# GpSimd's bulk loads of two attentions as single transfers in another order

## The reference

```python
# x: (8, 32, 32, 192), 12 heads of 16
x = x + conv_attn(group_norm(x))      # attention over all 1024 positions of an image:
#   scores = (q * scale) k^T + rel_h[..., :, None] + rel_w[..., None, :], softmax, times v, projection
t = x as tokens (8, 1024, 192)
t = t + attn(layer_norm(t))           # q k^T / sqrt(192), softmax, times v; 12 heads
t = t + ffn(layer_norm(t))            # each token by the expert of 16 with the largest logit
```

## Time and profile before

| what | us |
|---|---|
| median of 3 runs | 3230.5 (3227.85 to 3234.65) |
| span of the profiled execution | 3278.2 |
| PE busy | 2922.2 (89%) |
| DVE busy | 2439.8 (74%) |
| ACT busy | 1849.7 (56%) |
| POOL busy | 1061.6 (32%) |

### The profile page before, as it was taken

The page is one execution under the profiler, slowest core; times in us unless marked ns, Lnnn a source line. Parts: engine busy times, 40 slices in busy tenths (PEclk is TensorE's granted clock), DMA queues, the critical chain, the costliest instruction groups (busy, mean ns, idle before and its releaser), DMA issues. The chain is left out here.

```text
span 3278.2 us, 63755 instructions
## 1 busy us (share of the span) xinstructions
PE 2922.2 (89%) x17818; PEld 1147.0 (35%) x17818; DVE 2439.8 (74%) x4430; ACT 1849.7 (56%) x2379; POOL 1061.6 (32%) x1714
## 2 busy tenths in 40 slices
PE   5886999999999999977897999999999999871887
PEld 4664122222222222215652222222222222361666
DVE  4544899999999999933547999999999999451221
ACT  2433376667776677663440677777777777610332
POOL 0012233333333333213232333232333332155665
PEclk9776799999999999998995999999999999965777
DMA  6776554555445554433654622222222222350211
GB/s 126 219 237 184 104 103 98 100 110 107 102 101 100 111 103 100 90 61 121 206 160 98 124 72 70 72 75 75 73 76 75 70 71 63 97 89 12 58 54 35
DMA packets 222364, 327.92 MB, mean 100 GB/s; under 512 B 63820, under 2 KB 150550, under 8 KB 217650
## 3 DMA queue, kind: packets, MB, share of 16 engines
q0 software_dynamic: 79488, 202.00, 27.3%
q1 hardware_dynamic: 142772, 124.60, 14.5%
HBM read 217.71 MB, written 109.19 MB: 100 GB/s over the span
## 5 line engine op out<-in xcount | busy, mean ns | idle before, releaser
L458 ACT ACTIVATE a_probs<-a_psS 128x1024 f32<-128x1024 f32 x1536 | 1488.5, 1021 | 738.5 <-PE a_psS L371 734.0
L503 DVE TENSOR_REDUCE h_halfmax<-a_psR 128x1 f32<-128x512 f32 x1536 | 979.7, 686 | 73.5 <-PE a_psR L353 64.3
L503 DVE TENSOR_REDUCE a_halfmax<-a_psR 128x1 f32<-128x512 f32 x1536 | 984.2, 686 | 63.6 <-PE a_psR L353 54.5
L371 PE MATMUL a_psS<-a_qrows,a_krows 121*128 121x512 f16 (+1 forms) x3072 | 804.2, 383 | 44.8 <-DMA a_qrows<-relh 40.2
L382 PE MATMUL a_psO<-a_probs,a_v 128*32 128x512 f32 x6144 | 824.0, 609 | 1.2 <-ACT a_probs L458 1.2
L353 PE MATMUL a_psR<-h_kmax,h_qmax 64*128 64x512 f16 x1536 | 357.9, 405 | 40.8 <-POOL h_ident L39 40.1
L371 PEld LDWEIGHTS a_psS<-a_qrows,a_krows 121*128 121x128 f16 (+1 forms) x3072 | 241.8, 98 | 417.7 <-issue 161.5
L353 PE MATMUL a_psR<-a_kmax,a_qmax 64*128 64x512 f16 x1536 | 325.6, 393 | 1.8 <-DVE a_halfmax L503 1.4
L353 PEld LDWEIGHTS a_psR<-h_kmax,h_qmax 64*128 64x128 f16 x1536 | 81.9, 93 | 539.1 <-DVE h_halfmax L503 471.6
L353 PEld LDWEIGHTS a_psR<-a_kmax,a_qmax 64*128 64x128 f16 x1536 | 78.9, 93 | 490.4 <-DVE a_halfmax L503 460.1
L185 POOL DMA_DIRECT2D a_qrows<-qk x240 | 124.1, 517 | 264.5 <-PE a_psO L382 262.0
(11 more groups left out here) (185 smaller groups left out, 2755.2 us busy)
## 6 DMA issues: line engine op xcount, KB each, us to landing
a_qrows<-qk POOLq DMA_DIRECT2D x240, 128.0 KB, 4.2
qk<-p_half SPq DMA_DIRECT2D x96, 256.0 KB, 3.3
a_qrows<-rel POOLq DMA_DIRECT2D x96, 256.0 KB, 4.2
a_v<-v POOLq DMA_DIRECT2D x96, 256.0 KB, 3.1
a_krows<-qk POOLq DMA_DIRECT2D x168, 128.0 KB, 4.5
v<-p_v SPq DMA_DIRECT2D x36, 512.0 KB, 5.7
relh<-p_rel SPq DMA_DIRECT2D x48, 256.0 KB
attn<-a_out SPq DMA_DIRECT2D x96, 128.0 KB, 2.3
```

What stands on the lines that cost most here:

```text
L371: mm = nc.tensor.matmul(psS[:, (2 * n + j) % 4, :], K[buf][:, h, keys], A[buf][kt % NA][:, h, queries], start=True, stop=True)
L458: nc.scalar.activation(PT[:, blk % 2, 2 * pair:2 * pair + 2, :], psS[:, b0:b0 + 2, :], ACT.Exp, scale=scale).then_inc(exped, 1)
L503: nc.vector.tensor_reduce(mx[:, unit, half:half + 1], psR[:, slot, :], AX.X, ALU.max)\
```

## The change

The helpers that issued several transfers are split into one for each transfer, and `load_maxima` and `load` call them in another order, spread over more blocks. The transfers, their sizes, their semaphores and what PE waits for stay as they are.

| block | a1 before | a1 after | a2 before | a2 after |
|---|---|---|---|---|
| 0, 1 | 4, 2 maxima | 2 queries (L185 before) each | 2 maxima | 1 maxima query, 1 query or key |
| 2 | 2 maxima | 2 maxima, 2 queries | 2 maxima | as above |
| 3, 4 | 3 maxima | 2 maxima, 1 width | 2 maxima | as above |
| 5 | 3 terms | 2 maxima, 1 width | 2 maxima | as above |
| 6 | 3 terms | 1 maxima key, 1 width | 2 maxima | as above |
| 7 | 3 terms | 1 maxima key, 2 keys | 2 maxima | as above |
| 8 | 1 width, 1 height | 1 maxima width, 1 key, 2 heights | 1 query, 1 key | 2 maxima keys |
| 9 | 1 width, 1 height | 1 maxima width | 1 query, 1 key | 2 maxima keys |
| 10, 11 | 1 width | 1 maxima width | 1 query, 1 key | 2 maxima keys |
| 12, 13 | V | V | V | V |

```diff
@@ GpSimd of attention
-            def load_terms(s, buf, n):
+            def load_query(s, buf, c, n):
                 at = slice(HD * n, HD * n + HD)
-                for c in range(NA):
-                    pool.dma_start(A[buf][c][at, :, :], qk(s, TERMS[n][0], 0)).then_inc(loaded[buf], 16)
+                pool.dma_start(A[buf][c][at, :, :], qk(s, TERMS[n][0], 0)).then_inc(loaded[buf], 16)
+
+            def load_key(s, buf, n):
+                at = slice(HD * n, HD * n + HD)
                 pool.dma_start(K[buf][at, :, :], qk(s, TERMS[n][1], 1)).then_inc(loaded[buf], 16)
...
             def load_maxima(s, buf, blk):
 
+                if rel and 2 <= blk < 6:
+                    load_max_query(s, buf, blk % 2, (blk - 2) // 2, 0)
+                    load_max_height(s, buf, blk % 2, (blk - 2) // 2)
+                elif rel and blk in (6, 7):
+                    load_max_key(s, buf, blk % 2, 0)
+                elif rel and 8 <= blk < 12:
+                    load_max_width(s, buf, blk % 2, (blk - 8) // 2)
+                if not rel and blk < 8:
+                    load_max_query(s, buf, blk % 2, 0, blk // 2)
+                elif not rel and 8 <= blk < 12:
+                    load_max_key(s, buf, 0, blk - 8)
+                    load_max_key(s, buf, 1, blk - 8)
+
+            def load(s, buf, blk):
+
                 if rel:
-                    if blk == 0:
-                        load_max_terms(s, buf, 0, 0)
-                        load_max_terms(s, buf, 1, 0)
-                    elif blk < 5:
-                        load_max_rel(s, buf, blk % 2, (blk - 1) // 2)
+                    if blk < 3:
+                        load_query(s, buf, 0, blk)
+                        load_query(s, buf, 1, blk)
+                    elif blk < 7:
+                        load_width(s, buf, blk % 2, (blk - 3) // 2)
+                    elif blk == 7:
+                        load_key(s, buf, 0)
+                        load_key(s, buf, 1)
+                    elif blk == 8:
+                        load_key(s, buf, 2)
+                        load_height(s, buf, 0)
+                        load_height(s, buf, 1)
                 elif blk < 8:
-                    load_max_terms(s, buf, blk % 2, blk // 2)
-
-            def load(s, buf, blk):
-
-                if rel:
-                    if blk in (5, 6, 7):
-                        load_terms(s, buf, blk - 5)
-                    elif blk in (8, 9, 10, 11):
-                        load_rel(s, buf, blk % 2, (blk - 8) // 2)
-                elif blk in (8, 9, 10, 11):
-                    load_terms(s, buf, blk - 8)
+                    (load_query(s, buf, 0, blk // 2) if blk % 2 == 0 else load_key(s, buf, blk // 2))
                 if blk in (12, 13):
                     load_values(s, buf, blk - 12)
 
             make_identity(nc, pool, ident, const_done)
             for blk in range(12):
                 load(0, 0, blk)
-            for blk in range(BLK):
+            for blk in range(12):
                 load_maxima(1, 1, blk)
```

More of the change, by code:

```diff
@@ L181, in _, with load_width, load_height @@
         def _(pool):
-            def load_terms(s, buf, n):
+            def load_query(s, buf, c, n):
                 at = slice(HD * n, HD * n + HD)
-                for c in range(NA):
-                    pool.dma_start(A[buf][c][at, :, :], qk(s, TERMS[n][0], 0)).then_inc(loaded[buf], 16)
+                pool.dma_start(A[buf][c][at, :, :], qk(s, TERMS[n][0], 0)).then_inc(loaded[buf], 16)
+            def load_key(s, buf, n):
+                at = slice(HD * n, HD * n + HD)
                 pool.dma_start(K[buf][at, :, :], qk(s, TERMS[n][1], 1)).then_inc(loaded[buf], 16)
-            def load_rel(s, buf, c, half):
-                w, h = QR + WI * half, RH + 4 * half
+            def load_width(s, buf, c, half):
+                w = QR + WI * half
                 pool.dma_start(A[buf][c][w:w + WI, :, :], rel_w(s, half)).then_inc(loaded[buf], 16)
-                if half == 0:
-                    pool.dma_start(A[buf][c][RH:RH + 8, :, :], RLH[s, c].rearrange("i (k h) t -> (i k) h t", h=GH))\
-                        .then_inc(loaded[buf], 16)
+            def load_height(s, buf, c):
+                pool.dma_start(A[buf][c][RH:RH + 8, :, :], RLH[s, c].rearrange("i (k h) t -> (i k) h t", h=GH))\
+                    .then_inc(loaded[buf], 16)
             def load_values(s, buf, part):
@@ L197, in load_values, with load_max_query, load_max_key, load_max_width @@
                 pool.dma_start(V[buf][:, x, :, :], VN[s][:, x, :, :]).then_inc(loaded[buf], 16)
-            def load_max_terms(s, buf, r, n):
+            def load_max_query(s, buf, r, half, n):
                 of = slice(64 * r + HD * n, 64 * r + HD * n + HD)
-                pool.dma_start(AM[buf][0][of, :, :], qk_pair(s, TERMS[n][0], 0, r)).then_inc(loadedm[buf], 16)
+                pool.dma_start(AM[buf][half][of, :, :], qk_pair(s, TERMS[n][0], 0, r)).then_inc(loadedm[buf], 16)
+            def load_max_key(s, buf, r, n):
+                of = slice(64 * r + HD * n, 64 * r + HD * n + HD)
                 pool.dma_start(KM[buf][of, :, :], qk_pair(s, TERMS[n][1], 1, r)).then_inc(loadedm[buf], 16)
[L204 to L210, removed]
+            def load_max_width(s, buf, r, half):
+                of = slice(64 * r + HD, 64 * r + HD + WI)
+                pool.dma_start(AM[buf][half][of, :, :], RL[s, 0].rearrange("(k r p) t -> r k p t", p=2, r=2)[r])\
+                    .then_inc(loadedm[buf], 16)
+            def load_max_height(s, buf, r, half):
+                of = slice(64 * r + HD + WI, 64 * r + 64)
+                pool.dma_start(AM[buf][half][of, :, :],
                                RLH[s].rearrange("x i (k r p) t -> i r x k (p t)", p=2, r=2)[0, r, 4 * half:4 * half + 4])\
@@ L214, in load_maxima @@
             def load_maxima(s, buf, blk):
-                if rel:
-                    if blk == 0:
-                        load_max_terms(s, buf, 0, 0)
-                        load_max_terms(s, buf, 1, 0)
-                    elif blk < 5:
-                        load_max_rel(s, buf, blk % 2, (blk - 1) // 2)
-                elif blk < 8:
-                    load_max_terms(s, buf, blk % 2, blk // 2)
+                if rel and 2 <= blk < 6:
[10 more added lines that the diff above has]
+                    load_max_key(s, buf, 1, blk - 8)
             def load(s, buf, blk):
                 if rel:
-                    if blk in (5, 6, 7):
-                        load_terms(s, buf, blk - 5)
-                    elif blk in (8, 9, 10, 11):
-                        load_rel(s, buf, blk % 2, (blk - 8) // 2)
-                elif blk in (8, 9, 10, 11):
-                    load_terms(s, buf, blk - 8)
+                    if blk < 3:
[10 more added lines that the diff above has]
+                        load_height(s, buf, 1)
+                elif blk < 8:
+                    (load_query(s, buf, 0, blk // 2) if blk % 2 == 0 else load_key(s, buf, blk // 2))
                 if blk in (12, 13):
```

## The result

| | us |
|---|---|
| before, 4 runs beside it | 3229.8 (3227.9 to 3234.7) |
| after, 4 runs | 3263.7 (3257.3 to 3268.1) |
| ratio | 1.010 (1.0085 to 1.0116) |

The changed kernel is 34 us slower. Forecast were 23 us less; the time lies outside the range, and on the other side.

The account below looks back on a forecast made before the run. TensorE, busy nearly throughout both attentions, was taken as the bound, with a1 losing a height-row wait each step. Terms -48 + 6.6 + 15.4 + 3 = -23 us took 3230.5 to 3207.5 us, range 3186 to 3240.

Parts of the forecast that it names:

- Item 1: In a1, the scores' whole wait for the height rows goes: -48 us, bounds -40.2 and -48.
- The reading: Row transfers in a1 land 2.6 us after issue or 0.3 us after the last bulk load issued before, whichever is later.
- the table of landings per block: In a1, rows land 3.6 to 3.8 us after issue against 4.0, or at most 4.3 against 4.6.
- One reading: In a1, POOL's loads of blocks 7 and 8 were placed about 0.5 us after the scores of their own block.
- Item 2: Maxima's loads in a1, moved to blocks 2 to 11, delay block 13's scores 0.3 us a step: +6.6 us.
- Item 3: In a2, block 11's second maxima key load lands 0.7 us late for block 13: +15.4 us, plus +3 in weights' steps.
- the 3 us: In a2's steps 0 and 1, the experts' weights make the last maxima load later by 1.1 us more: +3 us.
- POOL isn't late anywhere: In both attentions, POOL's largest group, four loads, issues for 2.2 us of a 2.61 us block, so it costs nothing.
- the 2.15 us from block 11's first load to its deadline: Time from POOL's first load of block 11 to block 13's scores, read in a2 and used for a1 too.
- A: Rival: the maxima's loads at block 13 do not hurt, leaving the gain: 3182 to 3198 us; chance 0.10.
- B: Rival: a1's row transfers take turns with bulk packets in every busy block: +18 us, 3226 us; chance 0.17.
- C: Rival: a1's backlog survives until block 8, so the row wait stays: 3255.5 us; chance 0.16.

Follow-up runs that it names:

- e9: Before's order, with a1's three third-term loads moved from block 7 to blocks 11, 12 and 13: 3186.8 us, ratio 0.9859.
- e11: e4 with a1's two query loads of block 2 moved to block 6 and block 6's width load to block 9: 3236.5 us, ratio 1.0016.
- e5: Before's order, with a1's three third-term loads moved from block 7 to blocks 11, 12 and 14: 3197.5 us, ratio 0.9886.
- e8: e4 with a1's bulk width loads of blocks 3, 4 and 5 moved to blocks 9, 12 and 14: 3249.2 us, ratio 1.0056.
- e4: e1 with a1's last maxima width load moved from block 11 to block 10: 3210.2 us, ratio 0.9944.
- e1: After's order in a1 alone, before's order in a2: 3219.7 us, ratio 0.9956.
- e2: After's order in a2 alone, before's order in a1: 3266.7 us, ratio 1.0112.
- e7: e6 with one large a2 key load also moved from block 7 to block 12: 3241.1 us, ratio 1.003.
- e10: Before's orders, with the last of a2's maxima loads issued in block 12 instead of 7: 3348.6 us, ratio 1.0364.
- e6: e2 with one of block 11's two a2 maxima key loads moved to block 10: 3241.4 us, ratio 1.0018.

## Why the prediction was wrong, by its own steps

**Item 1, the height rows (-48 us): mis-sized, the mechanism right for the kernel before.** The price was right: e9 gets 47.8 us. It isn't the price of the waits alone, though. Where bare waits of 40.2 us stood against 46.2, the clock was in between: in before's a1 the granted clock fell to half for 3.4 us behind four of the 23 waits, as in step 3, behind a wait of 2.40 us:

```profile
536.70:540.10 3.40, 3.40 (x17) 1.19 (x16) 2.13 (x4) 1.34 (x2) 0.50 (x1) 0.50 0.24 55
```

Step 15, with a fall and a wait as long as its neighbours', is 1.2 us longer than they are, so the four are worth some 5 us (an estimate from that one step). The other profiles with the old order in a1 have three to seven such falls; e9 and after have none.

The reading was that a row transfer lands about 2.6 us after its issue, or 0.3 us behind the last bulk load issued before it. The first half holds (2.4 to 2.7 us with a light queue), the second where there is a backlog: the medians are 0.2 us in before's block 10 and 0.3 in e11's block 12 (landings read from the updates of the rows' semaphore in the trace). In after it was too short: the rows for blocks 5, 6, 7 and 11 landed 0.7, 1.9, 0.5 and 1.6 us behind that load. At block 11 of step 5 even a load issued 0.3 us behind the rows landed 1.2 us before them, so the order of issue isn't the whole rule; what the rest is, no run here shows.

The step that failed is therefore the table of landings per block. It set 3.6 to 3.8 us against a limit of 4.0, and at most 4.3 against 4.6, and called the whole wait gone. Measured medians of the rows issued in blocks 3, 5 and 9 were 4.24, 4.26 and 4.67 us, over their limits of 4.0, 4.0 and 4.6; those issued in block 8, where 3.8 stood, took 3.45. In step 5 the query load went out 0.15 us later behind the block's first load than assumed and the rows 0.1 earlier; the load took 3.8 us where 3.7 (3.5 and 0.2) stood, and the rows landed 0.4 us behind it where 0.3 stood: 4.2 us in place of 3.7. Tenths of a us decided, and margins of 0.2 to 0.4 us had been counted as certain.

The second part is the pause: the earlier trace rows show one step, and the trace of before has the pause ahead of block 1's loads in every third step. In before it costs nothing: five of the seven steps with it take 45.3 to 45.8 us, like the others, and the other two are those with a fall of the clock. In after such a step takes 1.16 us more (46.40 against 45.24 us), since the six loads of blocks 1 and 2 and the three of block 3 then come in a row; the rows issued in block 4, 3.7 us in the median, take up to 6.0. What is left of the 48 us: 27.7 in row waits and 8 in item 2's waits leave some 12, and a1 got 11 shorter, 4 of them by less waiting and the rest mostly by the four falls.

One reading was off without harm to the sum: loads of blocks 7 and 8 stand half a us behind the scores of blocks 8 and 9, not of their own block. e5 and e8 paid for it.

**Item 2, a1's maxima (+6.6 us): right.** The scores of block 13 cost 6.6 us over 21 steps, 9.4 at block 13 of which block 14 made up 2.8; e4 moved one load and got 5.9 back.

**Item 3, a2's maxima (+15.4 and +3 us): right for the ordinary step, wrong as a sum.** Ordinary steps lost 0.64 us, 14 us over 22 of them. The weights' steps lost 0.6 us, as any other, so the 3 us were not there. Missing was a term, and this is the step that failed here: in four of the steps GpSimd's pause falls ahead of block 11's loads. Those steps are 3.8, 6.9, 6.8 and 6.7 us longer than the ordinary 44.4, 24 us together. Two steps of the working let this through: "POOL isn't late anywhere" was read from groups of loads, not from the largest gap of the engine, and the 2.15 us from block 11's first load to its deadline were taken with an issuer that never stops. The clock wasn't in the sum at all.

**The sum.** Forecast -48 + 6.6 + 18.4 = -23. Measured by stages: a1 -11, which holds item 2, where -41 was forecast, and a2 +38, 14 by lateness and 24 by the four steps, where +18 was. That is 27 of 34 us; the other 7 are not placed, and e1 and e2, each against its own runs, give 23.

**The rivals.** A had no support: the waits at block 13 came. B named three of the four places of a1's waits (blocks 5, 6, 7; the fourth was 11 and not 10), and said 18 us where 27.7 were measured. The Trainium skill (DMA: Bandwidth & Descriptors, "Queues, rings and completion order") has each DMA engine take turns among its queues packet by packet. The earlier trace rows and e11, whose rows took 7 us behind the loads issued before them, don't show it; in after's step 5 packets of both queues moved in the same 1.7 us, and there it isn't ruled out. Whether turns are what made after's rows late by more than 0.3 us behind a load stays open. C's mechanism, a backlog to block 8, didn't come in after; its total (3255.5) was near for another reason. e11 is what C would look like.

## What to carry to other kernels

Before a load is moved later, compare its time from issue to need with its landing time plus the longest gap that its issuer ever shows in the trace, and not with the landing time alone; the gap is cheap until a deadline stands behind it. In this kernel a small transfer in another queue still landed behind most of the bulk loads issued just before it, so order these such that they don't land close to it: here three loads taken out of one group (e9) did what a reordering of thirty did not. Where a margin is a tenth of the quantity it protects, write both outcomes into the range.

## What the runs showed of the hardware that was not expected

- GpSimd pauses for 2.4 to 3.0 us between two instructions of its own in every kernel here: in a1 every third step (93 loads), in a2 of before after 88 and 94 loads in turn and in a2 of after every fourth step (104 loads), though a step's loads are the same 26. It isn't a plain count of loads or bytes, then, and e7 shows that it doesn't follow a single moved load. Nor is it code being loaded: between 650 and 1340 us of before, where six pauses lie, no packet moved in the instruction queues. The cause is open.
- TensorE's granted clock fell to half during or behind the wait at block 13 in all 22 loading steps of e10, where it waited 2.8 us or more, for 3.4 us in most and up to 13.7 us; in after behind all four waits that followed a pause, for 3.4 us once and 10.2 us three times. The waits of 0.7 us in the other steps of after's a2 brought none, the four of 1.2 us in e6's a2 none either, and one of the four of 1.2 to 1.3 us in e7's a fall of 6.8 us. Waits of 1.6 to 2.6 us for the height rows did either: four of 23 in before had a fall, always of 3.4 us, none of after's (up to 2.06 us), and the longest without one in any run was 2.50 us (a1 of e2). What decides between none, a short and a long fall is open.
- Loads of 128 KB into 16 partitions and of 256 KB into 32 both land about 1.1 us apart when they queue. Ten in a row behind step 9's pause in after (four large, six of the maxima) landed within 8.3 us, which leaves some 0.65 us for one of the maxima's, in place of half of 1.1: an estimate, as row transfers and an output transfer ran beside them.
